# Scalar chain of the hop phase: one instruction a step over 64 tiles, steps reordered

## What is computed

```python
hyper_head = expmap0(head_emb)
hyper_tail = expmap(tail_emb, hyper_head)
hyper_rel = expmap(rel_emb, hyper_head)
res = project(mobius_add(hyper_tail, hyper_rel))
res = logmap(res, hyper_head) + ricci * 1e-07
res = jax.nn.relu(res)
sums = jnp.zeros((n_entities, res.shape[-1]), res.dtype).at[head].add(res)
```

## Time and profile before

| | us |
|---|---|
| median of 3 runs | 19270.44 (19254.84 to 19276.73) |
| the profiled execution | 19271.95 |
| its span, first to last instruction | 19270.1 |
| VectorE busy | 14747.2 (77%) |
| GpSimd busy | 12260.2 (64%) |
| TensorE busy | 9310.3 (48%) |

### The profile page before, as it was taken

The page is one execution under the profiler, slowest core; times in us unless marked ns, Lnnn a source line. Parts: engine busy times, 40 slices in busy tenths (PEclk is TensorE's granted clock), DMA queues, the critical chain, the costliest instruction groups (busy, mean ns, idle before and its releaser), DMA issues. The chain is left out here.

```text
span 19270.1 us, 218526 instructions
## 1 busy us (share of the span) xinstructions
PE 9310.3 (48%) x50893; PEld 6358.9 (33%) x50894; DVE 14747.2 (77%) x25325; ACT 3949.6 (20%) x9903; POOL 12260.2 (64%) x12680
## 2 busy tenths in 40 slices
PE   0343325566666666655777763333243334344343
PEld 0333322232233233222333353333243334334333
DVE  8556668999999999998888832221488888688887
ACT  0111101111111111111000000000144444344443
POOL 0677876666666666663777727777376665566663
PEclk9999996666666666666888855555555655565555
DMA  5333221111111111112222211112532223233223
GB/s 212 76 83 72 69 71 29 25 27 26 25 27 26 25 26 27 25 25 24 29 30 29 28 13 26 26 26 26 66 75 70 73 74 62 69 75 75 68 73 55
DMA packets 1107684, 958.58 MB, mean 50 GB/s; under 512 B 758507, under 2 KB 874859, under 8 KB 1097292
## 3 DMA queue, kind: packets, MB, share of 16 engines
q0 software_dynamic: 368704, 436.55, 12.9%
q1 hardware_dynamic: 738316, 514.36, 10.4%
HBM read 736.74 MB, written 212.93 MB: 49 GB/s over the span
## 5 line engine op out<-in xcount | busy, mean ns | idle before, releaser
L1585 POOL DMA_INDIRECT tail<-ball,h_idx x3328 | 3493.3, 1050 | 2040.4 <-issue 1005.9
L835 PE MATMUL p_rad<-w_stack,hid_t 99*128 99x512 bf16 (+1 forms) x6656 | 2659.1, 551 | 2397.0 <-DVEq L932 1331.9
L905 DVE TENSOR_REDUCE red<-prod 128x96 f32<-128x1536 f32 x1664 | 2901.0, 1743 | 3.5
L1616 PE MATMUL h_sum<-head,h_hot 128*128 128x64 f32 x6656 | 1248.5, 375 | 3164.2 <-ACT head L1671 2993.5
L1616 PEld LDWEIGHTS h_sum<-head,h_hot 128*128 128x128 f32 x6656 | 1220.1, 287 | 3177.0 <-issue 3177.0
L343 POOL DMA_INDIRECT rec_a<-rec,slot x1600 | 1825.3, 1141 | 516.5 <-issue 487.2
L1229 POOL DMA_INDIRECT l_xg<-h_tab,l_idx x1664 | 1570.0, 944 | 835.9 <-issue 500.5
L835 PEld LDWEIGHTS p_rad<-w_stack,hid_t 99*128 99x128 bf16 (+1 forms) x6656 | 716.3, 122 | 4024.7 <-issue 3894.3
L1028 POOL DMA_INDIRECT l_xg<-x_tab,l_idx x1664 | 1570.2, 944 | 658.6 <-issue 493.3
L1042 PE MATMUL l_sum<-outer,l_hot 128*128 128x512 f32 x3328 | 1664.5, 665 | 531.2 <-DVEq L1087 531.2
L752 POOL DMA_INDIRECT l_xg<-in_x,l_idx x1664 | 1577.7, 948 | 522.9 <-issue 475.4
(11 more groups left out here) (408 smaller groups left out, 19410.8 us busy)
## 6 DMA issues: line engine op xcount, KB each, us to landing
hot_t<-rows_l SPq DMA_DIRECT2D x208, 512.0 KB
rec_a<-fill SPq DMA_DIRECT2D x128, 728.0 KB, 19.4
l_rec<-rec_a SPq DMA_DIRECT2D x104, 896.0 KB, 4.8
rhot_t<-rows_r SPq DMA_DIRECT2D x208, 384.0 KB
tail<-ball,h_idx POOLq DMA_INDIRECT x3328, 2.5
t<-in_type SPq DMA_DIRECT2D x100, 512.0 KB
l_xg<-in_x,l_idx POOLq DMA_INDIRECT x1664, 2.4
l_xg<-x_tab,l_idx POOLq DMA_INDIRECT x1664
```

What stands on the lines that cost most here:

```text
L835: ins = pe.matmul(p_rad[j % 3][:, h * 512:(h + 1) * 512], hid_t[j // 4 % 2][0:K3 + 3 * (1 - i), j % 4, i, :], w_stack[i][0:K3 + 3 * (1 - i ...
L905: ch.step(dve.tensor_reduce(red[q][:, j, :], prod[j % 3][:, :, :], AX, ALU.add))
L1585: pool.indirect_dma_start(tg[q][:, j, :], None, table[:, :], bass.IndirectOffsetOnAxis(ap=idx[q][:, j:j + 1], axis=0)).then_inc(gathered[q ...
L1616: ins = pe.matmul(p_sum[u % 2][:, j % BT // 2, :], hot[j // HP8 % 3][:, j % HP8, :], hg[:, j, 0:D], start=(j % 2 == 0), stop=(j % 2 == 1))
```

## The change

All 94 steps of the chain are concerned, and nothing else. `op` stays defined but isn't called. Each step becomes one instruction over all 64 tiles. `op_whole` waits, as `op` did, until the instruction before the last has finished; `op_tight` waits until the last one has. Seventy steps are `op_whole`, 23 are `op_tight`. Some steps change places, so that a step seldom needs what the one just ahead of it wrote. One step goes: the `ts` that doubles and adds 1 to `S2(16)` is folded into its neighbours (a factor 2 in one step, a 1 added in two). Waits for ScalarE and the other work between the parts stand where they stood. The diff, cut:

```diff
@@ -1772,145 +1772,150 @@
             def body(b, q, it, left):
                 h, t, r = hg, tg[q], rg
 
+                def run(f, z):
+                    n = z.stop - z.start
+
+                    def S(i):
+                        return sc[:, i, z]
+
+                    def S2(i):
+                        return sc[:, i:i + 2, z]
+
+                    def E(c):
+                        return h[:, z, c]
+
+                    def B2(a):
+                        return bc(a.unsqueeze(1), [P, 2, n])
+
+                    ch.step(f(S, S2, E, B2, z))
+
                 def op(f):
                     for half in range(2):
-                        z = slice(half * (W // 2), (half + 1) * (W // 2))
-
-                        def S(i):
-                            return sc[:, i, z]
-
-                        def S2(i):
-                            return sc[:, i:i + 2, z]
-
-                        def E(c):
-                            return h[:, z, c]
-
-                        def B2(a):
-                            return bc(a.unsqueeze(1), [P, 2, W // 2])
-
                         if ch.n > 1:
                             dve.wait_ge(chain_s, ch.n - 1)
-                        ch.step(f(S, S2, E, B2, z))
-
-                op(lambda S, S2, E, B2, z: dve.reciprocal(S2(INV), S2(NORM)))
-                op(lambda S, S2, E, B2, z: ts(S(13), E(T_S), TINY, None, ALU.max))
-                op(lambda S, S2, E, B2, z: dve.reciprocal(S(13), S(13)))
-
-                op(lambda S, S2, E, B2, z: tt(S2(NORM), S2(NORM), B2(S(13)), MUL_))
+                        run(f, slice(half * (W // 2), (half + 1) * (W // 2)))
+
+                def op_whole(f):
+                    if ch.n > 1:
+                        dve.wait_ge(chain_s, ch.n - 1)
+                    run(f, slice(0, W))
+
+                def op_tight(f):
+                    ch.sync()
+                    run(f, slice(0, W))
+
+                op_whole(lambda S, S2, E, B2, z: ts(S(13), E(T_S), TINY, None, ALU.max))
+                op_whole(lambda S, S2, E, B2, z: dve.reciprocal(S2(INV), S2(NORM)))
+                op_whole(lambda S, S2, E, B2, z: dve.reciprocal(S(13), S(13)))
+                op_tight(lambda S, S2, E, B2, z: tt(S2(NORM), S2(NORM), B2(S(13)), MUL_))
                 ch.sync()
                 dve.sem_inc(asked, 1)
                 if left:
                     compares(b + 1, 1)
                     compares(b + 1, 2)
                 dve.wait_ge(told, b * 4 + 1)
...
-                op(lambda S, S2, E, B2, z: ts(S2(16), S2(16), 2.0, 1.0, MUL_, ADD))
...
+                op_whole(lambda S, S2, E, B2, z: tt(S2(INV), S2(T), S2(INV), MUL_))
+                op_tight(lambda S, S2, E, B2, z: stt(out=S2(16), in0=S2(INV), scalar=2.0, in1=S2(HV), op0=MUL_, op1=MUL_))
+                op_whole(lambda S, S2, E, B2, z: tt(S2(T), S2(T), S2(T), MUL_))
+                op_whole(lambda S, S2, E, B2, z: tt(S2(16), S2(16), B2(E(T_ALPHA)), MUL_))
+                op_whole(lambda S, S2, E, B2, z: tt(S2(20), S2(T), B2(E(T_P2)), MUL_))
+                op_whole(lambda S, S2, E, B2, z: stt(out=S2(18), in0=S2(16), scalar=1.0, in1=S2(T), op0=ADD, op1=ADD))
+                op_whole(lambda S, S2, E, B2, z: stt(out=S2(20), in0=S2(16), scalar=1.0, in1=S2(20), op0=ADD, op1=ADD))
+                op_tight(lambda S, S2, E, B2, z: ts(S2(20), S2(20), TINY, None, ALU.max))
+                op_tight(lambda S, S2, E, B2, z: dve.reciprocal(S2(22), S2(20)))
+                op_tight(lambda S, S2, E, B2, z: tt(S2(A1), S2(18), S2(22), MUL_))
+                op_whole(lambda S, S2, E, B2, z: tt(S2(A2), S2(INV), S2(22), MUL_))
+                op_whole(lambda S, S2, E, B2, z: tt(S2(A1), S2(A1), B2(E(T_ALPHA)), MUL_))
+                op_whole(lambda S, S2, E, B2, z: tt(S2(A2), S2(A2), B2(E(T_S)), MUL_))
+                op_whole(lambda S, S2, E, B2, z: tt(S2(16), S2(A1), B2(E(T_SQ)), MUL_))
+                op_whole(lambda S, S2, E, B2, z: tt(S2(18), S2(A2), S2(HV), MUL_))
+                op_whole(lambda S, S2, E, B2, z: tt(S(25), S(A1 + 1), S(HV), MUL_))
+                op_whole(lambda S, S2, E, B2, z: tt(S(26), S(A2 + 1), tr[:, z], MUL_))
+                op_whole(lambda S, S2, E, B2, z: tt(S(24), S(17), S(19), ADD))
+                op_whole(lambda S, S2, E, B2, z: tt(S(25), S(25), S(26), ADD))
+                op_whole(lambda S, S2, E, B2, z: tt(S2(20), S2(A2), S2(VV), MUL_))
+                op_whole(lambda S, S2, E, B2, z: stt(out=S2(22), in0=S2(18), scalar=2.0, in1=S2(16), op0=MUL_, op1=ADD))
+                op_whole(lambda S, S2, E, B2, z: tt(S(24), S(24), S(A1), MUL_))
+                op_whole(lambda S, S2, E, B2, z: tt(S2(20), S2(20), S2(A2), MUL_))
+                op_whole(lambda S, S2, E, B2, z: tt(S2(22), S2(22), S2(A1), MUL_))
+                op_whole(lambda S, S2, E, B2, z: tt(S(25), S(25), S(A2), MUL_))
+                op_whole(lambda S, S2, E, B2, z: tt(S2(22), S2(22), S2(20), ADD))
+                op_whole(lambda S, S2, E, B2, z: tt(S(24), S(24), S(25), ADD))
+                op_whole(lambda S, S2, E, B2, z: tt(S(26), S(22), S(23), MUL_))
+                op_whole(lambda S, S2, E, B2, z: ts(S(25), S(24), 2.0, 1.0, MUL_, ADD))
+                op_whole(lambda S, S2, E, B2, z: ts(S(28), S(22), -1.0, 1.0, MUL_, ADD))
+                op_whole(lambda S, S2, E, B2, z: tt(S(26), S(25), S(26), ADD))
+                op_whole(lambda S, S2, E, B2, z: tt(S(27), S(25), S(23), ADD))
+                op_whole(lambda S, S2, E, B2, z: ts(S(26), S(26), TINY, None, ALU.max))
+                op_tight(lambda S, S2, E, B2, z: dve.reciprocal(S(25), S(26)))
+                op_tight(lambda S, S2, E, B2, z: tt(S2(27), S2(27), B2(S(25)), MUL_))
+                op_tight(lambda S, S2, E, B2, z: tt(S(29), S(28), S(24), MUL_))
+                op_whole(lambda S, S2, E, B2, z: tt(S2(22), S2(27), S2(22), MUL_))
+                op_whole(lambda S, S2, E, B2, z: stt(out=S(25), in0=tr[:, z], scalar=2.0, in1=S(VV), op0=MUL_, op1=ADD))
+                op_whole(lambda S, S2, E, B2, z: stt(out=S(29), in0=S(29), scalar=2.0, in1=S(22), op0=MUL_, op1=ADD))
+                op_whole(lambda S, S2, E, B2, z: tt(S(23), S(23), S(28), MUL_))
+                op_whole(lambda S, S2, E, B2, z: tt(S(29), S(29), S(27), MUL_))
+                op_whole(lambda S, S2, E, B2, z: tt(S(25), S(25), S(VV + 1), ADD))
+                op_whole(lambda S, S2, E, B2, z: tt(S(29), S(29), S(23), ADD))
+                op_whole(lambda S, S2, E, B2, z: ts(S(ROOTS_IN + 1), S(25), 1e-24, None, ALU.max))
+                op_whole(lambda S, S2, E, B2, z: ts(S(ROOTS_IN), S(29), TINY * TINY, None, ALU.max))
                 ch.sync()
                 dve.sem_inc(asked, 1)
                 if left:
                     relation_hots(1 - q, it + q)
                 dve.wait_ge(told, b * 4 + 2)
...
+                op_tight(lambda S, S2, E, B2, z: dve.reciprocal(S2(34), S2(ROOTS)))
+                op_tight(lambda S, S2, E, B2, z: ts(S(34), S(34), 1.0 - 0.004, 1.0, MUL_, ALU.min))
+                op_tight(lambda S, S2, E, B2, z: tt(S2(27), S2(27), B2(S(34)), MUL_))
...
+                op_tight(lambda S, S2, E, B2, z: ts(S(20), S(17), -2.0, 1.0, MUL_, ADD))
+                op_tight(lambda S, S2, E, B2, z: tt(S(21), S(20), S(21), ADD))
...
+                op_tight(lambda S, S2, E, B2, z: dve.reciprocal(S(23), S(21)))
+                op_tight(lambda S, S2, E, B2, z: tt(S(22), S(22), S(23), MUL_))
...
+                op_tight(lambda S, S2, E, B2, z: tt(S(30), S(30), S(25), ADD))
+                op_tight(lambda S, S2, E, B2, z: ts(S(SUB_IN), S(30), TINY * TINY, None, ALU.max))
                 ch.sync()
                 dve.sem_inc(asked, 1)
...
                 dve.wait_ge(told, b * 4 + 3)
...
+                op_tight(lambda S, S2, E, B2, z: ts(S(26), S(25), -1.0, 1.0, MUL_, ADD))
+                op_tight(lambda S, S2, E, B2, z: ts(S(25), S(25), 1.0, None, ADD))
...
+                op_tight(lambda S, S2, E, B2, z: tt(S(LOG_IN), S(25), S(27), MUL_))
                 ch.sync()
                 dve.sem_inc(asked, 1)
...
+                op_tight(lambda S, S2, E, B2, z: tt(S(26), S(26), E(T_S), MUL_))
                 if left:
                     compares(b + 1, 0)
                 dve.wait_ge(told, b * 4 + 4)
...
+                op_tight(lambda S, S2, E, B2, z: stt(out=S(26), in0=S(LOG), scalar=0.5, in1=S(26), op0=MUL_, op1=MUL_))
+                op_tight(lambda S, S2, E, B2, z: tt(S2(18), S2(18), B2(S(26)), MUL_))
...
                 ch.sync()
                 dve.sem_inc(asked, 1)
```

More of the change, by code:

```diff
@@ L1812, in body @@
[L1812 to L1825, removed]
@@ L1840, in body @@
[L1840 to L1845, removed]
-                op(lambda S, S2, E, B2, z: stt(out=S(25), in0=tr[:, z], scalar=2.0, in1=S(VV), op0=MUL_, op1=ADD))
@@ L1888, in body @@
[L1888 to L1889 removed]
+                op_tight(lambda S, S2, E, B2, z: dve.reciprocal(S2(34), S2(ROOTS)))
```

(36 more changed lines are left out.)

72 lines of the change are left out of this document (8 added, 64 removed).

## The result

The changed kernel takes 18998.34 us, the median of 4 runs (18981.46 to 19008.71); the kernel before takes 19264.67 us on the same chip, also the median of 4 (19254.84 to 19276.73). The ratio is 0.986, with a 95% interval of 0.985 to 0.988: 266 us faster, where 252 were forecast. The time lies inside the range, 20 us under the predicted 19018. The profiled execution of the changed kernel took 19008.71 us, against 19271.95 before, 263 us less.

What follows compares the result with a forecast made beforehand. VectorE's order of work was taken to bound the hop blocks. Savings of 7.36 us less 2.42 for tight waits and 0.10 for part ends gave 4.84 a block, 252 us over 52 blocks: 19018 us, range 18945 to 19090.

Steps and rivals of the forecast that it cites:

- VectorE's order of work sets the block: In the hops, VectorE's work sets the block's 99.4 us, so what the chain gives up comes off the block.
- The spacings: Start-to-start cost of the chain's whole steps: 0.135 us for one row, 0.20 for two, 0.25 or 0.32 behind tight waits.
- with head column, 5 and 7: Chain steps with a head column: five two-row ones save 0.35 us a block, seven one-row ones 0.49.
- The rule weighed: Skill's rule that each VectorE operation starts after the pipe empties; the prediction held that the halves' overlapping rows disagree.
- The sum: Chain's savings of 7.36 us a block less 2.42 for tight waits and 0.10 for part ends: 4.84 net.
- two-row `ts`: Chain's one remaining two-row `ts`, 0.22 to 0.15 us, and the one removed, 0.22: 0.29 us a block saved.
- tight waits, with the ends of parts: Cost in the chain: 21 waits at 0.115 us, 2.42 us a block, plus 0.10 for five parts' last instructions.
- Wide steps don't gain: Rival: the chain's two-row wholes cost what two halves did; 150 us gained, 19120 us; 6 in 100.
- The stream was short: Rival: the 71.5 us stall at the loop's head vanishes with 95 fewer instructions a block; 18947 us; 8 in 100.
- GpSimd binds: Rival: gathers slow to 1.5 us each and set a block of 97 us; 19145 us; 4 in 100.
- No overlap: Rival: all 93 chain steps start only when the one ahead finishes; 167 us slower, 19437 us; 3 in 100.

Runs made afterwards that it cites:

- e5_no_tight: Changed kernel's 93 steps on constant rows, each writing rows nothing reads, without tight waits; scalar formulas not computed; slower chip: 23504.0 us, ratio 0.9835.
- e4_two_row_halves: Changed kernel with its 29 two-row steps, reciprocals left out, run as two instructions each again; one-row steps stay whole: 19117.47 us, ratio 0.9924.
- e2_all_tight: Changed kernel with all 93 steps made to wait for the instruction just ahead: 19444.59 us, ratio 1.009.
- e1_halves: Changed kernel's new order and 93 steps, but each step in two instructions of 32 tiles again: 19255.59 us, ratio 0.9996.
- e10_same_rows_tight: Second run, on another slower chip, of the changed kernel's chain on constant rows with its 23 tight waits; scalar formulas not computed: 23971.14 us, ratio 0.990.
- e8_same_rows_tight: Changed kernel's chain on constant rows with its 23 tight waits; scalar formulas not computed; slower chip: 23684.47 us, ratio 0.990.
- the short kernels: Two runs of the constant-row chain without tight waits, minus 35 steps, the relation comparison and most of the head sum: 23135.23 and 23421.33 us.

## Why the prediction held

**VectorE's order of work sets the block.** Right. The spacings of the chain sum to 5.23 us a block less, the period is 5.1 to 5.4 us shorter, and the waits that are left have the releasers they had.

**The spacings.** The forecast gave 0.135 us for a one-row whole, 0.20 for a two-row one, 0.18 and 0.29 with the head column, 0.11 for a one-row `ts`, 0.25 behind a one-row step ahead of a tight one and 0.32 behind a two-row one. Over 52 blocks they are 0.135, 0.202, 0.181, 0.296, 0.110 (undisturbed), 0.25 to 0.26 and 0.32 to 0.33. The slope of 1.06 ns a column, read between 32-column halves of two rows and 1024 columns, held for the 128-wide step (1.05 from 64 to 128), and the head column's 1.7 ns nearly so (1.8). The reciprocal lasts 0.953 us at 128 columns and 0.553 at 64, 6.25 ns a column, near the 6.2 of the earlier trace rows.

**The rule weighed.** The prediction read only half of it. "The next op does not start until the 8-stage pipe empties", says the Trainium skill, "VectorE: DVE Perf Modes", section "The DRAIN you can't avoid", but the same section adds that "A next op that is not held starts earlier". With that exception there is no disagreement over the overlap: 64- and 128-wide fp32 instructions without a wait on the one just ahead start 0.135 and 0.20 us apart at durations of 0.21 and 0.28. What doesn't carry over is the section's measurement on a chain of copies, in which a semaphore after each "costs nothing extra": here each wait on the instruction just ahead costs 0.12 us, 446 us for 70 of them in 52 blocks.

**The sum.** It came out 5.23 us a block for 4.84: the savings were put too low, and so were the costs against them. In the table the savings are the spacings before less those in e5_no_tight, where the same steps run without waits:

| us a block | forecast | measured |
|---|---|---|
| two-row products and sums, 23 | 1.61 | 6.49 - 4.72 = 1.77 |
| one-row, 36 | 3.24 | 8.61 - 5.10 = 3.51 |
| with head column, 5 and 7 | 0.84 | 3.72 - 2.70 = 1.02 |
| one-row `ts`, 13 | 1.30 | 3.42 - 1.91 = 1.51 |
| two-row `ts` | 0.29 | 0.45 - 0.14 = 0.31 |
| reciprocals, 8 | 0.08 | 5.08 - 4.88 = 0.20 |
| saved | 7.36 | 8.34 (the rows round to 8.32) |
| tight waits, with the ends of parts | 2.52 | 2.82 |
| stalls of `ts`, not forecast | | 0.29 |
| net | 4.84 | 5.23 |

The savings were under-sized because the steps before were read from a few rows, not averaged over 52 blocks. Most one-row steps do take the 226 to 227 ns that were read, but L1832 takes 273, and L1896, ahead of ScalarE's third answer, and L1902, ahead of the fourth request, take 297 and 459; with a head column L1811 was read as 360 ns and takes 448. Then 0.095 was rounded to 0.09 for 36 steps, which is 0.18 us. The tight wait was put at 0.115 us and is 0.12, the ends were put at 0.10 us and are some 0.3, and the stalls had no term at all. So the forecast's closeness is in part luck: 0.98 us too little saved and 0.59 us too little paid cancel to 0.39 us a block, 20 us.

**The rivals.** *Wide steps don't gain*: e4_two_row_halves is 119 us slower than the changed kernel; they do. *The stream was short*: the stall at the loop's head is still 71.3 us with 95 instructions fewer a block, so their number doesn't cause it; what does stays open. *GpSimd binds*: it still waits 7.1 us for VectorE at 38 of its hand-overs. *No overlap*: not so here, but it is what e2_all_tight does, at the price forecast. The range's lower end rested on the second rival; without it 18975 would have done.

## What to carry to other kernels

In a chain of small VectorE instructions count the distance from start to start, not the durations: in this kernel VectorE was busy 14762.2 us in e2_all_tight and 14739.0 in e1_halves, and their times are 189 us apart. One instruction over twice the columns saves the fixed part of a start (0.09 us for 32 to 64 columns, 0.07 for 64 to 128), and a wait for the instruction just ahead costs 0.12 us, so merging halves pays as long as not too many steps need such a wait. As an estimate from three runs of these 93 steps, in halves (19255.59 us), whole with 23 tight (18998.34) and whole with 93 tight (19444.59): a straight line between the last two crosses the first at 63, about two thirds. Price a class of steps by its mean over all blocks; a few rows miss the odd ones.

## What had not been expected of the hardware

**A `ts` that starts late in a gather ends with the gather.** Two blocks of the changed kernel, VectorE and GpSimd in order of time:

```profile
14166.41 0.94 POOL L1585 DMA_INDIRECT tail<-ball,h_idx  x1 [0.30 <-issue]
...
14166.99 0.38 DVE L1860 TENSOR_SCALAR sc<-sc 128x64 f32<-128x64 f32 x1
14167.10 0.30 DVE L1861 TENSOR_SCALAR sc<-sc 128x64 f32<-128x64 f32 x1
```
```profile
14074.27 0.18 DVE L1860 TENSOR_SCALAR sc<-sc 128x64 f32<-128x64 f32 x1
14074.38 0.20 DVE L1861 TENSOR_SCALAR sc<-sc 128x64 f32<-128x64 f32 x1
14074.46 0.94 POOL L1585 DMA_INDIRECT tail<-ball,h_idx  x1 [0.30 <-issue]
```

In the first a gather runs when L1860 starts, and it takes 0.38 us; in the second L1860 falls into the gap between two gathers and takes 0.18. Of 52 instances 26 start beside a running gather and last 375 to 378 ns, and 26 don't and last 182 to 188. The kernel before has it too: its L1889 lasts 259 to 359 ns in 56 instances beside a gather and 173 to 182 in 48 without. But it isn't every gather under way: L1860 starts 0.58 us into its gather of 0.94 us. Of the changed kernel's one-row `ts` that read `sc`, the 296 that start in the first 0.49 us of a gather last 179 to 203 ns, as without one; the 108 that start 0.57 to 0.79 us into it end 0.01 to 0.06 us behind the gather's end, however long that makes them (194 to 378 ns). The `tensor_tensor` ahead of L1860, L1859, is 0.21 us either way. The Trainium skill, "SBUF — State Buffer", section "Who interferes with whom", tells of a port pair that VectorE and GpSimd share under an exclusive lock: `tensor_scalar` can take it whole, and then one of the two blocks fully; `tensor_tensor` has no such mode, though with both inputs in SBUF it contends with a GpSimd instruction that reads SBUF. The rows agree in that only the `ts` is longer and that it ends with the gather. They differ in that the first 0.49 us of a gather hold nothing up, where the section has the pair taken for the whole instruction. No run here shows that it is the port and not something else that goes with a gather. One line's durations (min, median, max) in the changed kernel, and the same step in e10_same_rows_tight, where GpSimd stands waiting while the chain runs:

```profile
L1860 DVE TENSOR_SCALAR sc<-sc x52: 182/282/378, 13885.7 to 18881.3; 128x64 f32<-128x64 f32 x52
```
```profile
L1861 DVE TENSOR_SCALAR sc<-sc x52: 182/183/186, 15959.9 to 23847.5; 128x64 f32<-128x64 f32 x52
```

The 0.29 us of stalls in the table is what the changed kernel's chain has over e8_same_rows_tight's, 22.55 to 22.26; 0.23 of it stands at five `ts` steps (L1807, L1846, L1849, L1861, L1903).

**The same program a quarter slower on some chips.** VectorE's chain runs at the same spacings there; it is TensorE whose instructions stand apart. Its groups of instructions in the hop (count, busy us, mean ns of one, idle us ahead of them by releaser), first the changed kernel, 14059.4 to 16230, then e10_same_rows_tight, 16000 to 19700:

```profile
L1616 PE MATMUL h_sum<-head,h_hot 128*128 128x64 f32 x2944 | 542.3, 370 | 1241.3 <-ACT head L1671 1159.9 <-DVEq L1942 80.2 <-issue 1.2
```
```profile
L1616 PE MATMUL h_sum<-head,h_hot 128*128 128x64 f32 x3168 | 701.2, 378 | 2158.5 <-ACT head L1671 1149.4 <-issue 1004.6 <-DVEq L1943 3.2
```

One matmul takes nearly as long, 370 and 378 ns, but ahead of them stand 1004.6 us in which TensorE waits for nothing that the profile shows, against 1.2. The granted clock of these stretches is 0.61 in the changed kernel and 0.54 in e10_same_rows_tight, but a lower clock that lengthens a matmul by 2% doesn't account for these gaps. VectorE has idle time there (15950 to 23400) that the profile gives to no engine:

```profile
DVE h_hot L1730 <- remote: 1326.3, 45, 39.6
```

By the kernel these are waits for `sum_done`, which TensorE raises (L1616). GpSimd waits for VectorE, and a block takes 150 us instead of 94. What delays TensorE's instructions on these chips no run here tells. It is why the short kernels couldn't answer their question, and why the experiments were compared only with what ran beside them.
